# Differential attention on one core: groups of four sub-heads replaced by pairs of two

## The reference, cut to what matters

```python
q = (x @ Wq).reshape(B, S, 2*H, d).transpose(0, 2, 1, 3) * scaling   # 32 sub-heads, d = 4
k = (x @ Wk).reshape(B, S, 2*H, d).transpose(0, 2, 1, 3)
v = (x @ Wv).reshape(B, S, H, 2*d).transpose(0, 2, 1, 3)
scores = where(causal_mask, -inf, einsum('bhqd,bhkd->bhqk', q, k))
probs = softmax(scores).reshape(B, H, 2, S, S)
attn = einsum('bhqk,bhkd->bhqd', probs[:, :, 0] - lam * probs[:, :, 1], v)
attn = attn * rsqrt(mean(attn*attn) + eps) * rms_w * (1 - LAMBDA_INIT)
x = layernorm(x + attn @ Wo)
r = sigmoid(xr @ W_r.T);  k_act = square(relu(xk @ W_k.T))   # xr, xk mix x with its predecessor
out = layernorm(x + r * (k_act @ W_v.T))
```

## Time and profile before

| what | value |
|---|---|
| median of 3 runs | 461.19 us (460.2 to 464.35) |
| time of the profiled execution | 459.95 us |
| its span, first to last instruction | 458.2 us |
| busy: TensorE, VectorE, ScalarE, GpSimd | 87%, 83%, 76%, 44% |
| period of one group in the middle of the run | 21.63 us |
| first exponential starts, last one ends | 63.0, 422.1 us |

### The profile page before, as it was taken

How to read it: one execution, slowest core, us unless ns; L and a number is a source line. 1 busy time by engine, 2 the same in 40 slices (tenths; PEclk the granted TensorE clock), 3 DMA queues, 4 the chain that set the end, 5 groups by cost and what they waited for, 6 DMA issues and landing times.

```text
span 458.2 us, 14401 instructions
## 1 busy us (share of the span) xinstructions
PE 396.4 (87%) x5191; PEld 167.3 (37%) x5191; DVE 382.1 (83%) x504; ACT 347.3 (76%) x687; POOL 199.4 (44%) x356
## 2 busy tenths in 40 slices
PE   5355669999999999999999999999999999899582
PEld 3241313343334333333333343433333434345452
DVE  2459998999999999999999999999999992334643
ACT  3360047989898999899998989898989998767333
POOL 7200011245555453637373646455554535553312
PEclk9795557999999999999999999999999999999877
DMA  5589020203030211212030202030202010000001
GB/s 135 207 303 340 23 93 2 97 1 95 4 94 6 91 43 50 54 39 93 0 93 0 93 0 93 0 93 1 92 10 83 1 49 3 1 0 24 24 1 46
DMA packets 20363, 28.40 MB, mean 62 GB/s; under 512 B 3936, under 2 KB 8928, under 8 KB 20208
## 3 DMA queue, kind: packets, MB, share of 16 engines
q1 hardware_dynamic: 19664, 27.44, 18.7%
q10 hardware_dynamic: 672, 0.59, 0.4%
HBM read 20.39 MB, written 9.47 MB: 65 GB/s over the span
## 4 chain that ended last, share of the span: by engine, by line
PE 46%; DVE 26%; ACT 13%; issue 11%; ACTq 2%; DMA 1%; POOL 1%; DVEq 0%; POOLq 0%
DVE part_max L1013 22%; PE acc L615 16%; ACT e_buf L924 10%; PE mx L530 9%; PE ex L584 7%; PE ex L627 2%; PE ex L646 1%; PE mx L615 1%; PE mx L712 1%; DMA x_tok<-in_L_attn_x 1%; PE mx L713 1%; ACTq L285 1%; PE mx L697 1%; PE mx L732 1%; DVE rest L973 1%
## 5 line engine op out<-in xcount | busy, mean ns | idle before, releaser
L924 ACT ACTIVATE e_buf<-ex 128x512 f32<-128x512 f32 x576 | 305.7, 599 | 44.8 <-PE ex L584 38.6
L1013 DVE TENSOR_REDUCE part_max<-mx 128x2 f32<-128x1024 f32 (+2 forms) x288 | 330.7, 1209 | 8.6 <-PE mx L530 7.3
L615 PE MATMUL acc<-e_buf,v_grp 128*32 128x256 f32 (+2 forms) x2200 | 177.6, 395 | 3.0 <-issue 2.8
L584 PE MATMUL ex<-qe,ke 26*128 26x512 bf16 (+3 forms) x768 | 145.4, 334 | 1.8 <-ACT e_buf L924 0.2
L530 PE MATMUL mx<-km,qm 29*128 29x128 bf16 (+3 forms) x1280 | 118.9, 273 | 23.1 <-DVE part_max L1013 21.1
L456 POOL TENSOR_SCALAR_AFFINE_SELECT e_buf<-e_buf 128x512 f32<-128x512 f32 x128 | 78.9, 635 | 131.0 <-ACT e_buf L924 131.0
L530 PEld LDWEIGHTS mx<-km,qm 26*128 26x128 bf16 (+1 forms) x1280 | 41.8, 94 | 145.6 <-DVE part_max L1013 135.9
L615 PEld LDWEIGHTS acc<-e_buf,v_grp 128*32 128x32 f32 x2200 | 43.7, 108 | 57.4 <-issue 51.6
L584 PEld LDWEIGHTS ex<-qe,ke 26*128 26x128 bf16 x768 | 44.3, 91 | 28.0 <-ACT e_buf L924 17.9
L440 POOL TENSOR_TENSOR r_rms<-sq_eps,minus_half 128x16 f32<-128x16 f32 x15 | 43.7, 2911 | 1.2
L419 POOL TENSOR_TENSOR r_lam<-r_den,lam_pair 128x32 f32<-128x32 f32 x15 | 4.0, 266 | 64.6 <-DVE r_den L1059 64.6
(11 more groups left out here) (134 smaller groups left out, 261.9 us busy)
## 6 DMA issues: line engine op xcount, KB each, us to landing
qm<-q_rows SPq DMA_DIRECT2D x16, 256.0 KB, 2.7
km<-k_rows SPq DMA_DIRECT2D x16, 256.0 KB, 2.9
qe<-q_rows SPq DMA_DIRECT2D x16, 256.0 KB, 3.1
ke<-k_rows SPq DMA_DIRECT2D x16, 256.0 KB, 3.3
q_rows<-part_q SPq DMA_DIRECT2D x6, 256.0 KB, 5.0
k_rows<-part_k SPq DMA_DIRECT2D x6, 256.0 KB, 4.9
q_rows<-part_q SPq DMA_DIRECT2D x6, 192.0 KB
k_rows<-part_k SPq DMA_DIRECT2D x6, 192.0 KB
```

What stands on the lines that cost most here:

```text
L584: scored = pe.matmul(ex[:, ex_slot(b, i) % EX_BANKS, col:col + w], ke[par][rows, P * kb:P * (kb + 1)], qe[par][rows, q1 - w:q1], start=col ...
L615: last = pe.matmul(bank[STRIP * j:STRIP * (j + 1), hi - w:hi], v_grp[par][:, kb, j // 2, shift:shift + STRIP], e_buf[:, k % ESLOTS, j, col ...
L924: nc.scalar.activation(e_buf[:, k % ESLOTS, 2 * p + i, :], ex[:, ex_slot(b, i) % EX_BANKS, :], ACT.Exp).then_inc(s["exped"], 1)
L1013: nc.vector.tensor_reduce(target, mx[m % 2][:].rearrange("p s (a b) -> p s a b", a=a), AX.X, ALU.max).then_inc(s["maxed"], 1)
```

## The change

A pair of two sub-heads takes the place of the group of four as unit of both passes. There are 32 pairs, n = 2g + pr, with 9 units of maxima and 9 bursts each. A unit and a burst have the sizes of before. The strips 2 and 3 now always hold the rows for the maxima and 0 and 1 those for the exponentials. EARLY stays 8, so 9 + 8 units come ahead of the first burst. The maxima of a pair are combined, split, turned (after burst 4), copied and written, and its sums taken (burst 3), turned (burst 6) and stored, each once a pair.

The sums of a burst are a whole quad of two sub-heads: of 512 query columns a strip holds two blocks of 128, 0 and 3 in one and 1 and 2 in the other, so that acc has 256 columns. The products of quads 1 and 8 come as 6 matmuls, those of quad 2 as 8, the others as 4; each is two instructions in the trace. The four transposes become two for each pair.

Tables and orders of the last group change with it: maxima end at burst 0 of pair 30; the first half of acc is complete at burst 6 of pair 31, is taken after burst 7 and turned and stored after burst 8. GpSimd's power and placing move from the end of `normalise` into `place_attn`, and VectorE does both `norm_attn` before `apply1(0)`, and `norm_ffn(1)` between `normalise_half(0)` and `place_half(0)`.

```diff
-NU = 2 * len(MAX_UNITS)
+NU = len(MAX_UNITS)
-NB2 = 2 * NQ
-ESLOTS = 5
+BLOCKS_OF = [(0, 3), (1, 2)]
+def sum_pieces(k):
+    pieces = []
+    for c, kb, col, w in QUADS[k]:
+        first = 4 - w // P
+        for ab, own in enumerate(BLOCKS_OF):
+            blocks = [q for q in own if q >= first]
+            if blocks:
+                cols = [col + P * (q - first) for q in blocks]
+                pieces.append((c, kb, ab, 2 - len(blocks), cols))
+    return pieces
-TAKE_AT, TURN_AT, MAXIMA_AT, INVERT_AT = 3, 6, 13, 9
+TAKE_AT, TURN_AT, MAXIMA_AT, INVERT_AT = 3, 6, 4, 1
...
-            sp.dma_start(qm[par][:], q_group[n]).then_inc(s_qkm[par], 16)
+            sp.dma_start(qm[pr][max_strips, :], q_pair[n]).then_inc(s_qkm[pr], 16)
...
+            def sum_burst(g, par, pr, k):
+                ...
+                for c, kb, ab, i, cols in sum_pieces(k):
+                    ...
+                    for jj in range(PAIR):
+                        strip = slice(STRIP * (2 * jj + ab), STRIP * (2 * jj + ab + 1))
+                        v = v_grp[par][:, kb, pr, shift:shift + STRIP]
+                        ...
+                        last = pe.matmul(out, v, e, start=first, stop=over, skip_group_check=True)
+                last.then_inc(s["summed"], 1)
...
-                for qb in range(4):
-                    last = pe.transpose(turned[:, P * qb:P * (qb + 1)], o_rows[par][:, P * qb:P * (qb + 1)],
-                                        identf[:])
+                for i in range(2):
+                    last = pe.transpose(turned[:, P * i:P * (i + 1)], o_rows[pr][:, P * i:P * (i + 1)], identf[:])
...
+            beside = {(0, 1): [(turn_attn, 0)], (0, 2): [(turn_attn, 1)], (0, 3): [(project, 0)],
+                      (0, 4): [(project, 1)], (0, 8): [(turn_x1, 0)], (1, 0): [(ffn_k, 0)], (1, 1): [(turn_x1, 1)],
+                      (1, 2): [(ffn_r, 0)], (1, 3): [(ffn_k, 1)], (1, 4): [(ffn_o, 0)], (1, 5): [(ffn_r, 1)],
+                      (1, 7): [(ffn_o, 1)]}
...
+                    if b == MAXIMA_AT and not (static and n + 1 >= NPAIR):
+                        copy_maxima(n + 1, MAXIMA_SLOT % EX_BANKS)
...
-                    if b == 11 and static and n == NG - 1:
+                    if b == 7 and static and n == NPAIR - 1:
                         take_half(0)
-                    if b == 13 and static and n == NG - 1:
+                    if b == 8 and static and n == NPAIR - 1:
                         store_half(0)
...
             norm_attn(0)
+            norm_attn(1)
             apply1(0)
-            norm_attn(1)
             apply1(1)
             invert(NG - 2, 0)
             square_k(0)
             norm_ffn(0)
+            square_k(1)
+            normalise_half(0)
+            norm_ffn(1)
+            place_half(0)
             apply2(0)
-            normalise_half(0)
-            square_k(1)
-            place_half(0)
-            norm_ffn(1)
```

463 lines of the change are left out of this document (239 added, 224 removed).

## The result

The kernel before took 461.21 us (median, 457.38 to 464.35), the changed one 463.77 us (461.32 to 465.93): a ratio of 1.0072, 95% interval 1.0043 to 1.0100, by the record's comparison (the two medians alone give 1.0056). Forecast were 456.7 us and a range of 449.5 to 463.5. Ratios here leave out executions over 1.5% above the fastest of their kernel, which are three of ten in b_turn7 and six of ten in b_late_turn7 (466.5 to 469.0 us). The profiled execution of the changed kernel took 463.41 us with a span of 461.6, 3.4 us longer than the span before.

What follows compares the result with a forecast made beforehand. VectorE was taken as the bound from 33 to 379 us, TensorE some 5% behind. Terms 1 to 3 gave +2.4, term 4 -7.5, term 5 -0.4 and +1.0: -4.5 from 461.19, so 456.7 us, range 449.5 to 463.5.

Steps and rivals of the forecast that it cites:

- Term 1: VectorE's combinations and splits: 32 at 0.38 us for 16 at 0.49, +4.3 us (0 to +7.8); reciprocals +0.7.
- Term 2: VectorE's stall at burst 6: 0.15 us in 29 pairs for 0.53 in 14 groups, -3.1 us (-7.4 to +8.0).
- Costed at nothing: More TensorE products, ScalarE copies, GpSimd masks and SyncE row loads: all hidden, with TensorE 0.15 us a burst to spare.
- Term 3: The start: first burst after 17 units instead of 26, at about 52.8 us; masked units at low clock +0.5 us.
- Term 4: From the last unit of maxima to the last sums: fewer bursts, a new wait of +4.7; -7.5 us (-10.5 to -4).
- Term 5: After the last sums: half-width copy and turn -0.4 us, TensorE's clock falling again +1.0 us (-1 to +3).
- C: No change: smaller chains save nothing (+3.5 us) and the tail's wait is at its upper end (+1.3); 461.5 us, chance 0.23.
- B: TensorE misses VectorE at burst 6 of every pair, 0.53 us instead of 0.15 in 29 pairs; 467.7 us, chance 0.11.
- A: No stall at burst 6 and cheap chains of 0.30 us; 449.8 us, chance 0.17.
- D: Row loads or written maxima land late and a pair's first scores wait, 0.5 us in 31 pairs; 472 us, chance 0.04.
- the period of two pairs: Sign in the middle of the run: two pairs take 21.6 to 22.2 us.
- The last unit of maxima: Sign at the end of VectorE's maxima: the last unit comes at 379 to 382 us.

Runs made afterwards that it cites:

- b_turn7: The kernel before with its sums turned behind burst 7 instead of 6; ratio 1.0004 (0.9950 to 1.0058).
- b_late_turn7: The kernel before with each chain one burst later and the sums turned behind burst 7; ratio 0.9973 (0.9884 to 1.0061).
- a_late4: The changed kernel with combination, cast and subtraction of each chain one burst later, the maxima still turned after burst 4; 476.44 us.
- a_tail: The changed kernel with another order at the end, all four last sums before `turn_attn(2)`; ratio 0.9987 (0.9941 to 1.0033) to the kernel before.
- a_unrolled: The changed kernel with VectorE's loop over groups written out; ratio 1.0065 (1.0020 to 1.0109) to the kernel before.
- b_unrolled: The kernel before with VectorE's loop over groups written out; ratio 1.0033 (0.9974 to 1.0093), profiled execution 463.29 us.
- a_extra_half: The changed kernel with a second half-size chain a pair on VectorE, on its own tile, behind the units of bursts 4, 5 and 6; 467.76 us.

## Why the prediction was wrong

**Term 1, the chains, is the step that failed.** Forecast was +4.3 with +0.7 for reciprocals, and at most +7.8 and +0.7; it was +11.0. The price of 0.49 for a full-size chain was right where it was read (0.50 in the first two groups). The saving by size was right too: 0.11 was taken, and the changed kernel's first chain costs 0.09 less. What failed is the step from there: "nothing saved, 0.49 a chain" took the price of one place as an upper bound for all others. In the middle of the run the same half-size chain finds two things that stood nowhere in the sum:
- VectorE's loop: 0.41 outside it and 0.53 inside, without masks and without a reciprocal. 0.1 of this is the register work behind the combination (0.24 to 0.14 with the loop written out). In the kernel before the reciprocal stood there and covered it.
- GpSimd's masks: chains now stand in bursts 0 to 2 of each pair, where the masks are, and no longer in bursts 9 to 11 of a group, where none are. That is 0.02 for a chain without a reciprocal and 0.15 for one with it.

The wait of the combination for the unit ahead, 0.12, is in the price at either size, which is one reason why half the size saves so little; a_late4's 0.13 for 0.35 shows how much the place makes.

An estimate from these numbers, over the 31 chains of the stream: with 0.38 a chain and 0.30 a reciprocal they should have taken 16.3 us, and took 21.7. The loop accounts for 24 x 0.11 = 2.6, the masks for 30 x 0.09 = 2.7, the size for 31 x 0.03 = 0.9, the one late unit for 0.5, and the reciprocals, at the 0.18 of the run without masks instead of 0.30, for -1.8: 4.9 of 5.4 us. The two new costs don't add up as simply when one is taken away, because units then come late from TensorE or a cast falls beside a mask: loop and masks each returned most of their gain.

The prediction weighed the Trainium skill, VectorE: DVE Perf Modes, section on the TRN2 errata: many small operations on SBUF each pay a fixed latency. The trace agrees in the main: half the elements took the reduction from 286 to 220 ns and, where no mask stood beside them, the cast from 193 to 165 and the subtraction from 175 to 163. By that rule alone the forecast would have been 460.2 us; the median was 3.6 us above even that.

**Term 2, the stall.** 0.15 a pair was forecast; it is 0.28 in even pairs and 0.03 in odd ones, 0.15 on average. The odd pair's reciprocal may give TensorE the time that it lacks in the even one; no run tests that. The cause that was named, ScalarE's copies ahead of the exponential waited for, is in part confirmed by the short copy; the price of 0.09 behind the turning of the maxima was not foreseen. Stalls and start together gave 1.5 us for 2.6.

**Costed at nothing.** TensorE was given 0.15 us to spare in a burst (0.98 against 1.13), which no row shows; by its busy time in the earlier trace rows, itself modelled, it is (21.63 - 20.67) / 18 = 0.05, hardly room for anything new. The more numerous products themselves cost 0.03 in two pairs (1.80 for 1.83), which is nothing measurable. ScalarE's copies were not free: they hold the turning of the maxima, 0.34 us of TensorE's time a pair, and became the second bound, since savings on VectorE turned up there (6.2 to 8.2 and 10.7 us). The loads of rows were hidden, though with less to spare than the 1.5 us said.

**Term 3** was right in its time: the first exponential at 53.7, in 52 to 54. **Term 4** gave -6.65 for -7.5, with a wait of 4.39 for 4.7. The last sums at the lower clock level make 0.6 to 0.8 us of what is missing (1.93 us for twenty products, which would be 1.34 at the pace of the sixteen just before and 1.13 at that of the 36 in a_tail); the rest is open. Had the trace before been one with the low stretch at 397 us, this row would read -9.3. **Term 5** gave -0.75 for +0.6, though the clock's low stretch did grow: granted 0.50 of full speed for 17.1 us behind the wait, for the 10 us of the earlier trace rows. TensorE's idle time ahead of the next chunk of attention fell from 3.60 to 2.79, which is as much as the whole row.

**The rivals.** C's time (461.5) was nearest, by luck: its premise, that chains save nothing by being smaller, does not hold (0.50 to 0.41), and the tail's wait was not at its upper end. B's stall of 0.53 did not come. A and D fell. One of the prediction's signs could not have told: the period of two pairs, 22.17, lies in its 21.6 to 22.2, while the sum itself comes to about 21.8 (an estimate: 1.9 us over some 15 periods). The last unit of maxima, at 388.6 for 379 to 382, did tell.

## What to carry to other kernels

The price of a short operation between long ones is a price of its place: what it must wait for, what overlaps it, what runs beside it. When a change makes it more frequent and moves it, bound its cost from above by a sum of the parts (the wait for the instruction ahead, its length, the restart of the next, what another engine does beside it), not by its price in the old place. Compare the same operation outside and inside a loop in one trace: here that alone splits the price. And where two engines are within 5% of each other, taking work from one shows mostly as a wait of the other; look for the wait before counting the gain. Where executions of one kernel fall into clusters, find out what a cluster is before reading a difference of its size.

## What the runs showed of the hardware

- A reduction of 64 elements to 16 costs VectorE 0.35 us behind the unit it reads from, and 0.13 behind one it doesn't (a_late4; 0.13 in b_late_turn7 for 128 to 32).
- A VectorE cast of 16 elements a partition took 165 ns without GpSimd's masks, 206 on average with them, and up to 0.38 us in single chains.
- Register work in VectorE's loop held the unit behind the combination by 0.1 us (0.24 to 0.14, a_unrolled), and held nothing where an independent reciprocal stood between the two (0.58 either way, b_unrolled).
- Half-size chains added to VectorE (0.25 us each where nothing covers them) raised two pairs by only 0.28, since one of the two went into a stall of 0.28 (a_extra_half).
- TensorE's clock was at its lower level for 6.9 us behind a wait of 1.56 us in one execution (b_unrolled) and stayed at the upper one behind the same wait in another (the kernel before); the low stretch made the stretch around it 2.6 us longer.
